# Context through the key weights first, then through centred query weights, in place of a folded weight product, and a new order of calls

## The reference, cut to what matters

```python
# B, T, S, D, F = 4, 1024, 154, 256, 1024
def reference(x, ctx, g_xattn, g_ffn, Wq, bq, Wk, bk, Wv, bv, Wo, bo, W1, b1, W2, b2):
    xn = layernorm(x)
    q = xn @ Wq.T + bq
    k = ctx @ Wk.T + bk
    v = ctx @ Wv.T + bv
    s = einsum('btd,bsd->bts', q, k) / 16
    s = keep the 32 largest of each row, -inf elsewhere
    x = x + tanh(g_xattn) * (softmax(s) @ v @ Wo.T + bo)
    h = relu(layernorm(x) @ W1 + b1)
    return x + tanh(g_ffn) * (h @ W2 + b2)
```

## Time and profile before

| | |
|---|---|
| median of 3 runs | 256.1 us (255.13 to 256.61) |
| the profiled execution | 256.24 us |
| its span, first to last instruction | 254.5 us |
| busy: TensorE, VectorE, POOL, ScalarE | 98%, 70%, 67%, 60% of the span |
| read from memory, written | 12.44 MB, 4.19 MB |

### The profile page before, as it was taken

How to read it: one execution, slowest core, us unless ns; L and a number is a source line. 1 busy time by engine, 2 the same in 40 slices (tenths; PEclk the granted TensorE clock), 3 DMA queues, 4 the chain that set the end, 5 groups by cost and what they waited for, 6 DMA issues and landing times.

```text
span 254.5 us, 6003 instructions
## 1 busy us (share of the span) xinstructions
PE 249.7 (98%) x2014; PEld 242.8 (95%) x2014; DVE 177.6 (70%) x744; ACT 152.4 (60%) x388; POOL 171.4 (67%) x264
## 2 busy tenths in 40 slices
PE   8999999999999999999999999999999999999995
PEld 7866898999999999999999999999999999999994
DVE  2798999999996398588757794679448795421042
ACT  2576677865664755575466565675566657555652
POOL 3457996897995893569636993669456964696300
PEclk9999999999999999999999999999999999999999
DMA  7992203103312210321120211001100001001011
GB/s 223 379 416 117 66 18 107 27 3 93 115 43 85 82 43 35 91 84 45 41 85 9 76 43 45 0 3 43 43 3 0 10 34 45 1 29 56 0 44 41
DMA packets 6878, 17.30 MB, mean 68 GB/s; under 512 B 800, under 2 KB 2368, under 8 KB 6592
## 3 DMA queue, kind: packets, MB, share of 16 engines
q1 hardware_dynamic: 6848, 16.93, 19.0%
HBM read 12.44 MB, written 4.19 MB: 65 GB/s over the span
## 4 chain that ended last, share of the span: by engine, by line
PE 90%; DVE 6%; POOL 2%; issue 1%; ACT 0%; POOLq 0%; ACTq 0%
PE y_ps L435 11%; PE y_ps L431 11%; PE z_ps L418 11%; PE z_ps L420 11%; PE y_ps L430 11%; PE z_ps L419 11%; PE sc_ps L345 6%; PE pt_ps L366 2%; PE att_ps L400 1%; PE att_ps L387 1%; DVE left L960 1%; PE att_ps L384 1%; PE att_ps L386 1%; PE y_ps L247 1%; PE att_ps L385 1%; DVE top L956 1%
## 5 line engine op out<-in xcount | busy, mean ns | idle before, releaser
L1279 POOL TENSOR_TENSOR hid_lo<-hid,hid_hi 128x256 fp32r<-128x256 f32 x120 | 87.0, 744 | 34.6 <-ACT hid L748 33.9
L747 ACT ACTIVATE hid_hi<-z_ps,small_in 128x256 fp32r<-128x256 f32 x128 | 60.6, 473 | 70.1 <-PE z_ps L420 69.8
L418 PE MATMUL z_ps<-x2nt_hi,w_hi 128*128 128x256 f32 x256 | 73.1, 285 | 0.0
L420 PE MATMUL z_ps<-x2nt_hi,w_lo 128*128 128x256 f32 x256 | 71.5, 279 | 0.0
L419 PE MATMUL z_ps<-x2nt_lo,w_hi 128*128 128x256 f32 x256 | 71.1, 278 | 0.0
L430 PE MATMUL y_ps<-w_hi,hid_hi 128*128 128x256 f32 x248 | 66.0, 288 | 0.0
L431 PE MATMUL y_ps<-w_lo,hid_hi 128*128 128x256 f32 x248 | 64.5, 282 | 0.0
L748 ACT ACTIVATE hid<-z_ps,small_in 128x256 f32<-128x256 f32 x128 | 60.4, 472 | 0.0
L435 PE MATMUL y_ps<-w_hi,hid_lo 128*128 128x256 f32 x248 | 50.4, 282 | 0.0
L418 PEld LDWEIGHTS z_ps<-x2nt_hi,w_hi 128*128 128x128 f32 x256 | 48.3, 188 | 0.0
L419 PEld LDWEIGHTS z_ps<-x2nt_lo,w_hi 128*128 128x128 f32 x256 | 48.2, 188 | 0.0
(11 more groups left out here) (155 smaller groups left out, 404.2 us busy)
## 6 DMA issues: line engine op xcount, KB each, us to landing
x_ring<-x SPq DMA_DIRECT2D x8, 512.0 KB, 4.5
out<-x SPq DMA_DIRECT2D x15, 256.0 KB, 2.0
xt_in<-x_t SPq DMA_DIRECT2D x7, 512.0 KB, 3.6
w_in<-w SPq DMA_DIRECT2D x2, 1024.0 KB, 10.8
wkq_in<-w_kq SPq DMA_DIRECT2D x1, 514.0 KB, 3.4
wvo_in<-w_vo SPq DMA_DIRECT2D x1, 513.0 KB, 6.6
xt_in<-x_t SPq DMA_DIRECT2D x2, 256.0 KB, 4.9
ctx_in<-ctx_t SPq DMA_DIRECT2D x1, 462.0 KB, 10.1
```

The source lines that it names most:

```text
L418: mm(dst, w1_hi[:, k, cols], hi[:, k, toks], start=k == 0, stop=False)
L420: last = mm(dst, w1_lo[:, k, cols], hi[:, k, toks], start=False, stop=k == KD - 1)
L747: func(hid_hi[:, c % RING, :], z_ps[c % 2][:, 0:2 * P], ACT.Relu, bias=b1[:, c:c + 1]).then_inc(hid_hi_made, 1)
L1279: nc.gpsimd.tensor_tensor(hid_lo[:, slot, :], hid[:, slot, :], hid_hi[:, slot, :], ALU.subtract).then_inc(hid_lo_made, 1)
```

## The change

The context goes through two stages of products in place of a folded weight. `project_ctx(h, m)` multiplies it with the key weights, `copy_ctx_keys` adds bk in the copy out of PSUM, so this is k itself. The query weights are centred by VectorE straight from SBUF, while that runs (`centre_queries`), and `make_keys` multiplies them with k. The score bias is bq against k (`weigh_keys`, `add_keys`). Gone are the fold, the key bias products and their copy. The key and query weights are two transfers now, and ScalarE issues the transfer of the first context as its own first instruction; the host lays the key weights out transposed. Beside it, the calls are rearranged on TensorE, ScalarE, VectorE and POOL, in the written-out part and in the loop.

```diff
-            sp.dma_start(wkq_in[:], w_kq).then_inc(kq_loaded, 16)
-            sp.dma_start(ctx_in[:, :, 0:S], ctx_t[:, :, 0:S]).then_inc(ctx_loaded[0], 16)
+            sp.dma_start(wk_in[:], w_k).then_inc(k_loaded, 16)
+            sp.dma_start(wq_in[:], w_q).then_inc(q_loaded, 16)
...
-            def fold_queries(m):
-
-                if m == 0:
-                    pe.wait_ge(kq_loaded, 16)
+            def project_ctx(h, m):
+
+                lo, hi = PIECES[h]
+                if h == 0:
+                    pe.wait_ge(k_loaded, 16)
+                else:
+                    pe.wait_ge(vals_copied, m + 1)
+                pe.wait_ge(ctx_loaded[h], 16)
                 for k in range(KD):
-                    last = mm(z_ps[m][:, 0:D + 1], wk[:, k, m * P:(m + 1) * P], wq_in[:, k, :], start=k == 0, stop=k == KD - 1)
...
+                    last = mm(z_ps[m][:, 0:hi - lo], wk[:, k, m * P:(m + 1) * P], ctx_in[:, k, lo:hi], start=k == 0, stop=k == KD - 1)
+                last.then_inc(ctx_keys_ps_made, 1)
 
             def make_keys(h, m):
                 lo, hi = PIECES[h]
                 if h == 0 and m == 0:
-                    pe.wait_ge(first_mt_made, 1)
-                    pe.wait_ge(mt_step, 3 * KD)
+                    pe.wait_ge(wq_step, 3 * KD)
                 if m == 0:
...
+                    pe.wait_ge(ctx_keys_made, KD * (h + 1))
                 for k in range(KD):
...
+                    last = mm(key_ps[h][m][:, 0:hi - lo], wq_centred[:, k, m * P:(m + 1) * P], ctx_keys[:, k, lo:hi],
                               start=k == 0, stop=k == KD - 1)
...
+            act.dma_start(ctx_in[:, :, 0:S], ctx_t[:, :, 0:S]).then_inc(ctx_loaded[0], 16)
...
+            def copy_ctx_keys(h, m):
                 lo, hi = PIECES[h]
...
+                act.wait_ge(k_loaded, 16)
+                act.wait_ge(ctx_keys_ps_made, KD * h + m + 1)
+                func(ctx_keys[:, m, lo:hi], z_ps[m][:, 0:hi - lo], ACT.Identity, bias=bk[:, m, :]).then_inc(ctx_keys_made, 1)
+
+            def weigh_keys(h):
+                lo, hi = PIECES[h]
+                act.wait_ge(q_loaded, 16)
+                act.wait_ge(ctx_keys_made, KD * h + 1)
+                func(keys_bq[:, 0, lo:hi], ctx_keys[:, 0, lo:hi], ACT.Identity, scale=bq[:, 0, :]).then_inc(keys_bq_made, 1)
...
             def centre_queries(m):
 
...
                 if m == 0:
...
+                    dve.wait_ge(q_loaded, 16)
+                nc.vector.bn_stats(wq_stats[:, m, :], wq[:, m, :]).then_inc(wq_step, 1)
+                dve.wait_ge(wq_step, 3 * m + 1)
+                nc.vector.bn_aggr(wq_mean[:, m, :], wq_stats[:, m, :]).then_inc(wq_step, 1)
+                dve.wait_ge(wq_step, 3 * m + 2)
+                nc.vector.tensor_scalar(wq_centred[:, m, :], wq[:, m, :], wq_mean[:, m, 0:1], None, ALU.subtract).then_inc(wq_step, 1)
```

TensorE's order, the written-out part as far as the first feed-forward parts and a turn of the loop:

```diff
             warm_up()
-            fold_queries(0)
-            fold_queries(1)
-            fold_key_bias()
+            project_ctx(0, 0)
+            project_ctx(0, 1)
             make_keys(0, 0)
             make_keys(0, 1)
             bias_scores(0)
             scores(0, 0)
             fold_values(0)
             fold_values(1)
+            fold_value_bias()
             scores(0, 1)
-            fold_value_bias()
             values_of(0)
             values_of(1)
-            make_keys(1, 0)
             transpose_picked(0, 0)
-            bias_scores(1)
+            project_ctx(1, 0)
+            project_ctx(1, 1)
             scores(1, 0)
             attend(0, 0)
+            make_keys(1, 0)
             make_keys(1, 1)
+            bias_scores(1)
             values_of(2)
+            transpose_x2n(0, 0)
             values_of(3)
-            transpose_x2n(0, 0)
             values_of(4)
             scores(1, 1)
             ffn_in(0, 0)
             ffn_in(0, 1)
+            transpose_picked(0, 1)
             values_of(5)
-            transpose_picked(0, 1)
             ffn_in(0, 2)
             ffn_out(0, 0)
             ffn_in(0, 3)
+            attend(0, 1)
             ffn_out(0, 1)
-            attend(0, 1)
             ffn_in(0, 4)
             ffn_in(0, 5)
+            scores(2, 0)
+            ffn_in(0, 6)
             ffn_out(0, 2)
-            ffn_in(0, 6)
             ffn_out(0, 3)
+            transpose_x2n(0, 1)
+            transpose_picked(1, 0)
+            ffn_in(0, 7)
             ffn_out(0, 4)
...
                 ffn_in(u, 3)
+                ffn_out(u, 0)
                 ffn_in(u, 4)
-                ffn_out(u, 0)
                 ffn_out(u, 1)
+                ffn_out(u, 2)
+                transpose_picked(a, 0)
                 ffn_in(u, 5)
+                ffn_in(u, 6)
+                ffn_out(u, 3)
+                attend(a, 0)
+                ffn_in(u, 7)
+                ffn_in(u + 1, 0)
+                transpose_picked(a, 1)
+                ffn_out(u, 4)
                 if has_n:
                     scores(n, 0)
```

ScalarE early, and VectorE and POOL, where the prediction speaks of them:

```diff
+            weigh_wo()
             take_tanh()
-            weigh_wo()
+            fold_wvo()
             exps(0, 0)
-            fold_wvo()
             scale_value_bias()
             copy_values(0)
-            weigh_ctx(1)
             copy_rest(0, 0)
             copy_values(1)
             w1_to_hi(0)
+            copy_ctx_keys(1, 0)
             pt_to_hi(0, 0)
+            copy_ctx_keys(1, 1)
             w2_to_hi(0)
+            weigh_keys(1)
             copy_keys(1, 0)
...
             pt_to_lo(0, 0)
+            topk_round(0, 1, 0)
             first_residual()
-            topk_round(0, 1, 0)
+            add_keys(1)
+            topk_round(0, 1, 1)
             normalise_second()
...
                 pick(a, 0)
-                if n + 1 < GROUPS:
-                    stats_x(n + 1)
+                output(g - 1, 1)
                 scale_scores(a, 1)
                 topk_round(a, 1, 0)
                 topk_round(a, 1, 1)
                 topk_round(a, 1, 2)
+                pt_to_lo(a, 0)
                 topk_round(a, 1, 3)
-                output(g - 1, 1)
-                pt_to_lo(a, 0)
...
             stack_first_rest()
-            scale_b2()
             add_wo()
+            value_bias_to_lo()
             rstd_x(0, 1)
-            value_bias_to_lo()
             place_other_rests()
             first_values_to_lo()
             w1_to_lo(0)
+            scale_b2()
```

More of the change, by code:

```diff
@@ L26, with gated_block @@
 LAST = len(PARTS) - 1
-def gated_block(nc, x, x_t, w_kq, ctx_t, w_vo, small, w1, w2, out):
+def gated_block(nc, x, x_t, w_k, w_q, ctx_t, w_vo, small, w1, w2, out):
     f32, f32r = mybir.dt.float32, mybir.dt.float32r
@@ L535, in _ @@
+            ffn_out(1, 1)
+            ffn_out(1, 2)
             ffn_in(2, 0)
+            ffn_out(1, 3)
+            attend(1, 1)
             ffn_in(2, 1)
             ffn_out(1, 4)
-            ffn_out(1, 5)
-            attend(1, 1)
             ffn_in(2, 2)
             ffn_in(2, 3)
+            ffn_out(1, 5)
             ffn_out(1, 6)
             ffn_out(1, 7)
+            ffn_out(2, 0)
+            ffn_out(2, 1)
             ffn_in(2, 4)
+            transpose_picked(2, 0)
+            transpose_x2n(1, 1)
@@ L559, in _ @@
+            ffn_out(2, 6)
             ffn_in(3, 2)
+            attend(2, 1)
+            ffn_out(2, 7)
             ffn_in(3, 3)
-            transpose_picked(2, 1)
-            ffn_out(2, 5)
+            ffn_in(3, 4)
+            ffn_out(3, 0)
+            ffn_in(3, 5)
             scores(3, 1)
-            ffn_out(2, 6)
-            ffn_out(2, 7)
-            ffn_in(3, 4)
-            attend(2, 1)
-            ffn_in(3, 5)
+            ffn_out(3, 1)
+            ffn_in(3, 6)
+            ffn_out(3, 2)
@@ L795, in _ @@
             relu(1, 1)
+            exps(1, 1)
             relu(1, 2)
@@ L1055, in _ @@
             first_stats_x(0)
-            add_ctx(0)
+            add_keys(0)
             first_stats_x(1)
@@ L1109, in _ @@
             topk_round(2, 1, 3)
+            output(0, 1)
+            stats_x(3)
             pick(2, 1)
+            pt_to_lo(2, 0)
             x2nt_to_lo(1, 1)
-            pt_to_lo(2, 0)
+            stats_x(4)
+            residual(2, 0)
             scale_scores(3, 0)
-            stats_x(4)
-            output(0, 1)
-            residual(2, 0)
             pt_to_lo(2, 1)
@@ L1345, in _ @@
             hid_to_lo(3, 7)
+            rstd_x(4)
             add_b2(2, 1)
```

290 lines of the change are left out of this document (110 added, 180 removed).

## The result

The changed kernel takes 257.04 us (median of 12 runs, 255.99 to 257.84), the kernel before 255.78 (12 runs on the same chip, 254.96 to 256.62): ratio 1.0048, 95% interval 1.003 to 1.0067. Its profiled execution took 256.76 us with a span of 255.0, against 256.24 and 254.5 before.

The account below looks back on a forecast made before the run. TensorE, busy 98% of the span, was taken to bound the kernel. The terms -1.15 + 3.1 - 1.55 - 0.09 = +0.3 us on 256.24 gave 256.5 us, range 254.9 to 258.2.

Parts of the forecast that it names:

- Part 1: Start to first scores: fold and key bias out, project_ctx(0) in; make_keys at 7.15 instead of 8.62, -1.45 us.
- Part 2: At fold_values: TensorE ready at 9.85 waits for w_vo until 10.4, so the lead shrinks from 1.6 to 1.15 us.
- Part 3: Projection of the other 462 context columns, project_ctx(1): eight new TensorE passes, +3.1 us.
- Part 4: From 11.54 to 41.81: added work fills the waits for vo_bias_lo, x2n (twice) and pt_lo, -1.55 us.
- The sum: Whole kernel: -1.15 + 3.1 - 1.55 - 0.09 = +0.3 us, on 256.24.
- the place of the transpose: At transpose_x2n(0, 1): scores(2, 0) in (1.05), a transpose and an ffn_out out (1.14), -0.09 us.
- Part 5: Reordering after 42 us: same calls, turns stay 28.2 us if none waits, costed at nothing.
- The rival of the loop: Each turn waits for pt_lo at attend(a, 0), 0.35 x 5 = 1.75 us slower, 258.2 us; chance 0.09.
- The late clock: TensorE idles from 6.3 to 7.15 and stays at 1.2 GHz through scores(0, 0): +1.8 us, 258.3; chance 0.08.
- The price of a late one: First context lands at 5.4 because the second queue does not help: +0.3 us more, 256.8; chance 0.06.
- Not absorbed: VectorE and POOL path keeps its waits (0.34 + 0.18 + 0.66), total +1.5 us, 257.7; chance 0.10.

Follow-up runs that it names:

- gated pair: Kernel before and changed kernel, both with 16 warm-up products and the first fold or projection held until transposed x landed: 259.86 and 260.91 us.
- hybrid_split: Changed kernel, but key weights folded with query weights for the other 462 columns, add_keys(0) first, POOL's w2_lo subtractions in pieces of 256: 255.99 us.
- keys_first: Changed kernel with VectorE doing add_keys(0) before first_stats_x(0): 257.03 us, ratio 1.0039 to the kernel before.
- after_again: The changed kernel, unaltered, measured and profiled a second time: 256.88 us, ratio 1.0031 to the kernel before.
- half_projection: Changed kernel with project_ctx(1) doing four of its eight passes (keys of three batch elements wrong): 255.29 us, ratio 0.9983 to the kernel before.
- before_new_loop: Kernel before with only its loop bodies on TensorE, ScalarE, VectorE and POOL replaced by the changed kernel's: 256.58 us, ratio 1.0024.
- before_gated: Kernel before with 16 warm-up products in place of 7 and the fold held until transposed x landed: 259.86 us, ratio 1.0166.
- ctx_on_sp: Changed kernel with the first context issued by SP, second in its order, not by ScalarE: 259.4 us, ratio 1.0142 to the kernel before.
- after: The changed kernel itself in its first measurement and profile: 257.04 us, ratio 1.0048 to the kernel before.

## Why the prediction was right, and where its steps were off

The forecast was 256.5 us, no change most likely; measured, 257.04 and 256.88. Against its own basis, one profiled execution, it is near too: 256.76. It is right partly by luck, since its terms miss in both directions. By stage, changed kernel less kernel before, in us (from the starts of the calls named; in the gated pair from the first pass of fold or projection):

| | forecast, by its starts | the profiled pair | the gated pair |
|---|---|---|---|
| up to fold_values | -1.15 | -1.80 | -1.46 |
| to ffn_in(0, 0) | +2.1 | +2.14 | +2.12 |
| to the transpose of x2n | -0.9 | 0.00 | +0.03 |
| behind it | 0 | +0.17 | +0.18 |
| sum | +0.1 | +0.5 | +0.9 |

- **Part 1, up to the first scores.** make_keys was to start at 7.15 and started at 6.91, scores at 8.8 and started at 8.59. The query weights landed at 4.64, not 4.9, and the two halves of the centring took 2.0 us, not 2.25, so that the copy of the projected context on ScalarE ended last. The rows:

```profile
4.64 0.43 DVE L867 BATCH_NORM_STATS2 wq_stats<-wq_in 128x6 f32<-128x256 f32 x1 [3.14 <-DMA wq_in<-w_q]
...
6.26 0.35 DVE L871 TENSOR_SCALAR wq_centred<-wq_in,wq_mean 128x256 f32<-128x256 f32 x1
```

- **Part 2, the lead of 1.15 us.** The wait that this step rests on did not take place in the profiled execution. fold_values began at 9.74, not 10.4, and 1.15 us behind scores(0, 0), the same distance as in before, where w_vo had landed a microsecond earlier. w_vo was issued at 3.52 and took 6.1 us, not 6.6, so it was there at 9.6, just in time. The lead was 1.80, all of it. The mechanism is real where w_vo lands later: fold_values then waits, 0.57 us in hybrid_split and 0.2 in keys_first. The 1.33 us of lead in after_again have another cause, the wait for x.

- **Part 3, +3.1 us.** 3.10 measured, 16.53 to 19.63. How much of it counts is a matter of Part 4: half_projection shows that some 0.7 us of it fill a wait for pt_hi.

- **Part 4, waits filled.** The three waits for vo_bias_lo and x2n are gone, as said. From fold_values to ffn_in(0, 0) the sum gave 19.7 us and the trace 19.74. From there to the transpose of x2n it gave 11.8 and the trace 12.67, as much as in before. That is the step that failed: "a transpose, attend, scores(2, 0)" were put down without waits. The transpose at 31.14 comes 0.18 late and attend 0.43 at 35.78, because two picks of 0.31 us took 1.5 and 1.4 beside POOL. Where the first of them is short, as in after_again, the stretch takes 11.75, which is the sum's 11.8. The trace of before had that price to be read, as a pick of 1.38 us at 30.39; the forecast puts two picks at 0.8 us together.

- **The sum.** It takes -0.09 for the place of the transpose into the total, though an order of calls is no time by itself; without it the terms give +0.4. Its own starts, 41.9 against 41.81, give +0.1.

- **Part 5, nothing after 42.** 28.20 us a turn, no wait. The rival of the loop did not come. before_new_loop lost 0.6 us with another part before the loop, 0.30 of it idle at an attend, once and not in each turn.

- **The basis.** A sum on one execution takes over that execution's clock. The level rose at about 6.7 in it. With an earlier rise the fold is up to 1.15 us shorter (before_gated), while make_keys of the changed kernel came only 0.14 earlier in after_again, whose projection was 0.72 shorter. The medians of before in the five sets, 255.47 to 256.11, all lie below the 256.24 that I built on. So the difference of medians, 0.9 to 1.3 us, is larger than the 0.5 between the two profiled executions; the gated pair gives 1.05 by its medians. In the table the gated pair differs from the profiled one by 0.34 us in the first row, where the clock and the landings act, and by next to nothing in the others. The picks' 0.9 in the third row is the larger part of what the forecast missed, against the 0.3 to 0.65 that the first row gave more than forecast. This division rests on single traces. That it also explains the medians is argued, not shown. No run puts the new algebra together with the old order of the written-out part, so the cost isn't divided between the two either.

- **The other rivals.** The late clock did not come with one idle stretch of 0.66 us (6.25 to 6.91: the four passes of make_keys behind it took 0.60 in all), and came with two in ctx_on_sp. The context was there at 4.19. The price of a late one was named as 0.3; with the query weights and the clock that went with it, ctx_on_sp lost 2.4. "Not absorbed" named the waits at x2n, which are gone; what cost the time is a new wait, at the attend between them.

## What to carry to other kernels

Passes added to an engine that is busy 98% of the span cost their time, less the waits that they fill, and each of these waits should be named and priced, with what the other engines do beside the instructions that it waits for. An experiment that takes work away can move another part of the kernel as well: compare it stage by stage before the end is put down to the work. A chain bound by a fixed transfer or another engine can't use an early clock, while a chain of passes can; so the same edit is worth another amount at another moment of the rise, and one profile of before shows only one of them. When a variant is ahead early and level at the end, lay the starts of a repeated call side by side over the whole span before looking for one large wait.

## What the runs showed of the hardware that I had not expected

- A VectorE instruction of 0.31 us with two inputs in SBUF lasts 1.4 to 1.5 us beside a POOL subtraction of 1.31 us, and 0.83 to 0.96 beside pieces of 0.75. Where both start within 0.05 us of each other it was 1.5 us in after and 0.31 in after_again, the same program.
- Moving one transfer of 154 KB from ScalarE's queue into SP's made the next one, of 257 KB, land 2.35 us later in the one trace of ctx_on_sp.
- The same filled turn of the loop takes 28.18, 28.27 or 28.33 us in kernels whose loops have the same calls and whose tiles are laid out otherwise, without a wait in the trace.
- The column of the granted clock reads 1.00 also where TensorE's passes run at the 1.2 GHz level: in the changed kernel's stage from 4 to 6 us the starts of the projection's passes of 154 columns are 0.25 to 0.30 us apart, against 0.131 later. The level is to be read from the starts of the passes.

```profile
4.00:6.00 2.00, 2.00 (x10) 2.00 (x9) 1.29 (x4) 0.39 (x1) 0.00 (x0) 1.00 0.80 293
```
